# Layer 0 experts: TensorE's first six dense batches in a loop of three turns, and the second biases added in one pass

## The reference

```python
final_e = _route(tokens, router_w)          # top 1 of 8 experts, at most 640 tokens each;
out = jnp.zeros_like(tokens)                # what is dropped goes to expert 0
for e in range(E):
    h = jax.nn.relu(tokens @ W1[e] + b1[e])
    y = h @ W2[e] + b2[e]
    out = out + jnp.where((final_e == e)[:, None], y, 0.0)
x = x + out
```

## Time and profile before

| | |
|---|---|
| runs shown | 1693.18, 1695.10, 1690.64 us; median 1693.18 |
| the profiled execution | 1690.63 us, its span 1688.8 us |
| PE | 1403.0 us busy (83%) |
| DVE | 1086.1 us (64%) |
| ACT | 809.3 us (48%) |
| POOL | 666.7 us (39%) |
| mean granted TensorE clock | 0.939 of full speed |

### The profile page before, as it was taken

How to read it: one execution, slowest core, us unless ns; L and a number is a source line. 1 busy time by engine, 2 the same in 40 slices (tenths; PEclk the granted TensorE clock), 3 DMA queues, 4 the chain that set the end, 5 groups by cost and what they waited for, 6 DMA issues and landing times. The chain is left out here.

```text
span 1688.8 us, 44889 instructions
## 1 busy us (share of the span) xinstructions
PE 1403.0 (83%) x14646; PEld 1041.3 (62%) x14646; DVE 1086.1 (64%) x3491; ACT 809.3 (48%) x2363; POOL 666.7 (39%) x1261
## 2 busy tenths in 40 slices
PE   4888888866869979999999999969899999965671
PEld 2666666655557746666666666647677777744561
DVE  3888888847410067787777777756777777762223
ACT  2555555521223347777777777744343344402330
POOL 1344444420523424444444444432243344343552
PEclk9999999975879979999999999989999999978996
DMA  5555633300111222212212222200000000002225
GB/s 189 165 171 171 221 106 106 108 1 1 40 40 44 62 80 73 72 57 72 72 57 71 72 63 65 69 3 1 2 13 9 13 13 13 12 27 64 77 81 157
DMA packets 95508, 115.46 MB, mean 68 GB/s; under 512 B 12418, under 2 KB 76938, under 8 KB 95312
## 3 DMA queue, kind: packets, MB, share of 16 engines
q1 hardware_dynamic: 88752, 102.55, 19.6%
q0 software_dynamic: 6688, 12.07, 2.2%
HBM read 78.97 MB, written 37.32 MB: 69 GB/s over the span
## 5 line engine op out<-in xcount | busy, mean ns | idle before, releaser
L1615 ACT ACTIVATE c_pr<-c_pS,c_nm 128x257 f32<-128x257 f32 x512 | 238.2, 471 | 97.8 <-DVE c_nm L1751 97.8
L1751 DVE TENSOR_REDUCE c_nm<-c_pS 128x1 f32<-128x257 f32 (+1 forms) x384 | 173.3, 505 | 42.6 <-PE c_pS L1495 42.4
L1499 PE MATMUL c_pT<-cst,c_pr 128*128 128x128 f32 x1024 | 162.8, 284 | 0.0
L2085 ACT ACTIVATE s_k<-s_pK 128x512 f32<-128x512 f32 x128 | 76.4, 597 | 179.4 <-PE s_pK L1965 177.7
L1965 PE MATMUL s_pK<-s_hT,AH 128*128 128x128 f32 x1024 | 138.7, 285 | 0.5 <-ACT s_hT L2080 0.5
L1965 PEld LDWEIGHTS s_pK<-s_hT,AH 128*128 128x128 f32 x1024 | 125.1, 196 | 21.4 <-ACT s_k L2085 18.2
L1499 PEld LDWEIGHTS c_pT<-cst,c_pr 128*128 128x128 f32 x1024 | 111.3, 142 | 37.7 <-issue 37.7
L1986 PE MATMUL s_pM<-BH,s_uT 128*128 128x128 f32 x1024 | 123.9, 280 | 4.9 <-DVE LG L2234 4.9
L1986 PEld LDWEIGHTS s_pM<-BH,s_uT 128*128 128x128 f32 x1024 | 119.7, 196 | 7.6 <-DVE LG L2234 7.6
L1760 DVE COPY c_prT<-c_pT 128x512 f32<-128x512 f32 x128 | 88.5, 691 | 23.9 <-PE c_pT L1499 18.5
L1495 PE MATMUL c_pS<-c_ks,c_qq 32*128 32x257 f32 x1024 | 92.7, 431 | 13.1 <-POOL c_qq L1667 8.6
(11 more groups left out here) (354 smaller groups left out, 3328.6 us busy)
## 6 DMA issues: line engine op xcount, KB each, us to landing
rows_in<-c_blank SPq DMA_DIRECT2D x32, 520.0 KB, 3.1
a_ctxT<-in_ctxT SPq DMA_DIRECT2D x32, 514.0 KB, 3.6
c_ctxT<-in_ctxT SPq DMA_DIRECT2D x128, 128.5 KB, 2.2
a_ctxN<-in_ctxR SPq DMA_DIRECT2D x32, 512.0 KB, 4.2
f_back<-rows_out SPq DMA_DIRECT2D x24, 256.0 KB, 5.2
f_hb<-rows_in SPq DMA_DIRECT2D x39, 130.0 KB
f_w<-in_f_w SPq DMA_DIRECT2D x16, 256.0 KB, 3.5
rows_in<-a_zero SPq DMA_DIRECT2D x7, 322.5 KB, 4.6
```

The source lines that it names most:

```text
L1499: mm = pe.transpose(pT[:, c, j, :], pr[:, b % 2, j, c * P:(c + 1) * P], k("ident"))
L1615: act.activation(pr[:, b % 2, c, :], pS[:, c, 0:S], ACT.Exp, bias=nm[:, c:c + 1], accum_out=den[:, b % 2, c:c + 1]).then_inc(e_ready.sem, 1)
L1751: dve.tensor_reduce(nm[:, c:end], pS[:, c:end, 0:S], AX.X, ALU.max, negate=True).then_inc(max_ready.sem, 1)
L2085: act.activation(k2[:, c * HK:(c + 1) * HK, :], pK[:, c % 2, :, :], ACT.Copy).then_inc(k_ready.sem, 1)
```

## The change

The two edits are independent of each other.

First, PE's dense batches 0 to 5 are no longer written out. A hardware loop of three turns (`pe.Fori`) runs `two_batches(i)`: up 2i, up 2i+1, down 2i, down 2i+1. The waits and the columns of `HT_all` are now computed from the loop's register. So that the first turn needs no special case, ACT adds 4 to `up_ready` and DVE adds 8 to `added` at the start, and the waits count from there. Batches 6 and 7, at the end, use the same body once, written out.

Second, DVE no longer builds `bias` and adds it: 32 fused instructions do `X[g] += b2[0] * MASK[g]`, one for each group. The wait for all of them moves into `dense`.

```diff
-        bias = sb("bias", [P, G, D])
...
+        FREE_HIDDEN, FREE_SUMS = NF, 2 * TG
...
             def up(n):
                 for c in range(NF):
-                    m = n * NF + c
-                    if m >= 4:
-                        pe.wait_ge(up_ready, m - 3)
-                    pe.matmul(pH[:, m % 4, :], w1[:, 0, c * P:(c + 1) * P],
-                              HT_all[:, n * TG:(n + 1) * TG, :].rearrange("p g t -> p (g t)"), start=True, stop=True).then_inc(up_done, 1)
-
-            def down(n):
-                pe.wait_ge(up_ready, (n + 1) * NF)
-                if n > 1:
-                    pe.wait_ge(added, (n - 1) * TG)
+                    pe.wait_ge(up_ready, n * NF + (c + 1 - NF + FREE_HIDDEN))
+                    pe.matmul(pH[:, c, :], w1[:, 0, c * P:(c + 1) * P],
+                              HT_all[:, bass.ds(n * TG, TG), :].rearrange("p g t -> p (g t)"), start=True, stop=True).then_inc(up_done, 1)
+
+            def down(n, half):
+                pe.wait_ge(up_ready, n * NF + (NF + FREE_HIDDEN))
+                pe.wait_ge(added, n * TG + (FREE_SUMS - TG))
...
+            def two_batches(i):
+                for half in range(2):
+                    up(i * 2 + half)
+                for half in range(2):
+                    down(i * 2 + half, half)
+
             def dense(first, end):
-                up(first)
-                for n in range(first, end):
-                    if n + 1 < end:
-                        up(n + 1)
-                    down(n)
+
+                if first == 0:
+                    with pe.Fori(0, end // 2) as i:
+                        two_batches(i)
+                else:
+                    two_batches(first // 2)
...
+            act.sem_inc(up_ready, FREE_HIDDEN)
...
+            dve.sem_inc(added, FREE_SUMS)
             dve.wait_ge(b2_loaded, 16)
             for g in range(G):
-                dve.tensor_scalar(bias[:, g, :], b2[:, 0, :], MASK[:, g, 0:1], None, ALU.mult).then_inc(bias_ready, 1)
-            dve.wait_ge(bias_ready, G)
-            dve.tensor_tensor(X[:, :, :], bias[:, :, :], X[:, :, :], ALU.add).then_inc(bias_ready, 1)
-            dve.wait_ge(bias_ready, G + 1)
+                dve.scalar_tensor_tensor(X[:, g, :], b2[:, 0, :], MASK[:, g, 0:1], X[:, g, :], ALU.mult, ALU.add).then_inc(bias_ready, 1)
...
                     dve.wait_ge(down_done, n + 1)
+                    dve.wait_ge(bias_ready, G)
```

More of the change, by code:

```diff
@@ L1074, in up @@
                 for c in range(NF):
-                    m = n * NF + c
-                    if m >= 4:
-                        pe.wait_ge(up_ready, m - 3)
-                    pe.matmul(pH[:, m % 4, :], w1[:, 0, c * P:(c + 1) * P],
-                              HT_all[:, n * TG:(n + 1) * TG, :].rearrange("p g t -> p (g t)"), start=True, stop=True).then_inc(up_done, 1)
-            def down(n):
-                pe.wait_ge(up_ready, (n + 1) * NF)
-                if n > 1:
-                    pe.wait_ge(added, (n - 1) * TG)
+                    pe.wait_ge(up_ready, n * NF + (c + 1 - NF + FREE_HIDDEN))
[4 more added lines that the diff above has]
+                pe.wait_ge(added, n * TG + (FREE_SUMS - TG))
                 for t in range(TG):
                     for c in range(NF):
-                        mm = pe.matmul(pY[:, n % 2, t, :], hid[:, n % 2, c, t * P:(t + 1) * P], w2[:, 0, c, :],
+                        mm = pe.matmul(pY[:, half, t, :], hid[:, half, c, t * P:(t + 1) * P], w2[:, 0, c, :],
                                        start=(c == 0), stop=(c == NF - 1))
                 mm.then_inc(down_done, 1)
-            def dense(first, end):
-                up(first)
-                for n in range(first, end):
-                    if n + 1 < end:
-                        up(n + 1)
-                    down(n)
+            def two_batches(i):
[3 more added lines that the diff above has]
+                    down(i * 2 + half, half)
+            def dense(first, end):
+                if first == 0:
[3 more added lines that the diff above has]
+                    two_batches(first // 2)
             def turn(e):
@@ L1119, in sorted_down @@
                 if e == 1:
-                    pe.wait_ge(added, BEFORE * TG)
+                    pe.wait_ge(added, BEFORE * TG + FREE_SUMS)
                 else:
@@ L1218, in _ @@
             all_phases(dense, sorted_)
-            dve.wait_ge(added, G)
+            dve.wait_ge(added, G + FREE_SUMS)
             for n in range(NB):
```

## The result

The changed kernel is slower: 1697.89 us, median of 11 runs, against 1690.64 for the kernel before (11 runs). The ratio is 1.0047, 95% interval 1.0033 to 1.0061. The profiled execution took 1698.59 us, its span 1696.8 us, 8.0 us more than before's span.

What follows compares the result with a forecast made beforehand. A PE stall, not an engine's limit, was taken to bound the kernel, then `f_h`: `turn(1)` 15.6 us earlier, less 2.8 for the clock, is 12.8, so 1690.6 becomes 1677.8; 2.55 more for the median gives 1680.4 us, range 1674 to 1697.

Steps and rivals of the forecast that it cites:

- an announcement that came late: Dense batches: PE's `down_done` of batch 2 seems to have reached ACT and DVE 22 us late.
- `f_h` as the next bound: Before `turn(1)`: without the stall, the wait for the load of `f_h` ends last, at 480.5 us with the change.
- rival B: Dense part: the stall is in the recorded execution only, so `f_h` and the bias decide; 1691.1 to 1697.5 us, chance 0.10.
- I take the stall to be tied to PE's code arriving amid the scatter: Stall in `down(3)`: PE's code loads go with it; the loop needs none between first turn and exit, gaining 18.2 us.
- the 18.2 us of gain on PE: PE's dense part: without the stall it would end at 477.9 us instead of 496.09.
- rival A: Dense part: the stall belongs to the scatter or PE's semaphores, not its code, and stays; 1690 to 1695 us, chance 0.20.
- the same work on PE: Loop body: the order of up and down inside a turn leaves PE's work unchanged and adds no wait.
- The bias on POOL: POOL's scatters: 4.08 us of delay removed, 2.0 us added by the fused instructions; POOL ends 2.1 us earlier.
- The clock: Start of `turn(1)`: after idling from 477.9 to 480.5 us PE runs at half clock, losing 2.8 us.
- The range: Whole kernel: from 1674 us over rivals A and B to 1697, leaving out C and the edges.
- Rival C: Loop's head: the loop makes PE load code more often, 18.2 us per load that draws a stall; 1711 us, chance 0.08.

Runs made afterwards that it cites:

- half_scatter: The kernel before with 16 of the 32 scatters to rows_in left out: 1674.41 us, ratio 0.9899.
- paced8: The kernel before, with POOL waiting before scatters 8, 16 and 24 until all earlier ones have landed: 1688.80 us, ratio 0.9969.
- no_bias: The kernel before with the second bias of expert 0 left out of the result, so DVE never holds POOL: 1701.42 us, ratio 1.0045.
- bias_only: The kernel before with the fused bias alone, PE's batches written out as before: 1696.91 us, ratio 1.0034.
- gate2: The kernel before, with the train of scatters held back until PE's second dense batch is done: 1704.06 us, ratio 1.0057.
- after_paced8: The changed kernel with POOL waiting before scatters 8, 16 and 24 until all earlier ones have landed: 1691.79 us, ratio 0.9983 to the kernel before.
- seven: The kernel before with waits before scatters 8, 16 and 24, and seven dense batches ahead of the sorted experts, not six: 1684.31 us, ratio 0.9938.

## Why the prediction was wrong

- **What bounds the kernel.** Right: a stall from 464.5 to 482.1 that cost 18.2 us, with an announcement that came late, and `f_h` as the next bound. half_scatter measured its worth (18.3 us), and paced8 showed that next bound. half_scatter also rules out rival B, the stall in the recorded execution only: its median is 16.5 us lower.
- **The step that failed** is "I take the stall to be tied to PE's code arriving amid the scatter". It rested on one q8 load before the stall. The loop did silence q8, and the stall stayed; half_scatter has all the code and no stall. So the 18.2 us of gain on PE, the term on which the sum stood, did not come: the stage became 5.2 us longer. What the runs show in its place is that the stall goes with the length of POOL's uninterrupted train. That was rival A, at 0.20, and its own argument ("the stall ended 3.5 us after POOL's last scatter") should have weighed more than the coincidence: it holds in all eight stalled traces, with 2.6 to 4.5 us.
- **Rival A's time**, 1690 to 1695, was too low as well, because it priced the change at nothing while the stall lasts. The order inside a turn was costed as "the same work on PE". It is, but a stall divides work into what is before it and what is behind, and `up(4)` changed sides: +4.0 us behind the stall in the profile. It takes both edits for that. The loop alone made the stage 1.1 us longer and the order alone 1.7, since there the rest of `down(3)` was done within the stall.
- **The bias on POOL.** I took 0.3 us for each of seven scatters, 2.1 us in all gained. In fact one scatter was held until the train of 32 had ended (6.26 us, against 5.05 by the long addition). POOL's part from first to last scatter grew from 44.8 to 46.2 us: 1.35 lost, inside my bounds. What I missed altogether is that the pause itself was useful, since it sets back the onset: with no pause (no_bias) the stage was 9.4 us longer. In bias_only, where the pause ends 2.1 us sooner, it was 2.2 us longer; its medians differ by 6.0 us, more than the trace explains.
- **The clock** term came to nothing in the change, since there was no wait. In paced8 it showed: `turn(1)` took 2.50 us instead of 1.28, and the third `turn` began 20.3 us after the first instead of 17.8, so the term of 2.8 was near.
- **The range** reached to 1697.0; the time was 1697.9. It was counted from a median of 1693.2 for the kernel before, which over 11 runs was 1690.6, so the loss was larger than the two numbers suggest. Rival C, the slower one, had the wrong mechanism: code loads did not increase.
- The rule that a taken branch out of the loaded window forces a load (Trainium skill, Runtime: NRT & Kernel Launch, Instruction fetch mechanics) was not put to a test that would show it: q8 was silent through the loop's turns and its exit, up to `turn(1)`, so no load of that kind stands in the trace. The Trainium skill's GPSIMD Engine Reference, Key points, says that GpSimd contends with VectorE instructions of two SBUF inputs; the traces agree, and add the price. One scatter is held to the end of the whole back-to-back train; the two before it, which also began beside that train, took 1.10 and 1.01 us. Why those got through no run tells.

## What to carry to other kernels

A stall in which an engine waits for nothing that the profile shows should be tested by removing the suspected neighbour's work before anything is built on a cause; here one variant with half the scatters settled it. Where a stall can't be avoided, count what stands in front of it and what behind: reordering that is free on a busy engine may not be free around a stall. Where a long train of indirect DMAs runs beside dense TensorE work, try pauses: in this kernel one before every eighth scatter removed the stall. Something that holds POOL up for 4 us may already be such a pause.

## What the runs showed of the hardware

- Beside an uninterrupted train of indirect scatters (one each 1.28 us), PE, busy with the dense batches, starved 12.7 to 15.3 us after the train began (gate2) or was last interrupted, in seven traces; 17.5 us in no_bias, whose train began with PE at half clock on wide matmuls. With no stretch of scatters so long (half_scatter, paced8, after_paced8) it did not, and seven shows one gap of 0.28 us. Singles came through at multiples of 0.7 us, until 2.6 to 4.5 us after the end of the last scatter.
- PE's semaphore increments seem to be late before PE itself slows: in paced8, where PE never slows, DVE heard of batch 3 some 4 us after PE's last matmul of it, within a pause of 2.1 us.
- What it is that backs up between PE and POOL, and whether PE's rate or POOL's alone sets the onset, no run here tells. The scatters came at one spacing in all runs, so their number and the time without a pause aren't told apart either. Nor was it tested whether the recording of the execution has a part in the stall.
- GpSimd held by back-to-back VectorE instructions of two SBUF inputs: up to 5.05 us by one of 4.42 us, 5.5 to 6.5 us by 32 in 8.5 us, each time until 0.8 to 0.9 us after the last.
